# First layer's attentions on one Trainium2 core: score and value products in longer stretches of one kind

## The reference, cut to what matters

```python
def _attn(xq, xc, Wq, Wk, Wv, Wo, bo):
    ...
    scores = jnp.einsum('bnhd,bshd->bhns', q, k) * scale
    attn = jax.nn.softmax(scores, axis=-1)
    out = jnp.einsum('bhns,bshd->bnhd', attn, v).reshape(B, N, HEADS * D_HEAD)
    return out @ Wo + bo
...
x = _attn(_ln(x, g1, b1), _ln(x, g1, b1), Wq1, Wk1, Wv1, Wo1, bo1) + x
x = _attn(_ln(x, g2, b2), context, Wq2, Wk2, Wv2, Wo2, bo2) + x
```

## Time and profile before

| what | value |
|---|---|
| median of the timed runs | 3437.53 us |
| span of the profiled execution, first to last instruction | 3432.5 us |
| PE busy | 3202.0 us, 93% of the span |
| DVE busy | 2266.1 us, 66% |
| ACT busy | 1823.8 us, 53% |
| POOL busy | 1087.6 us, 32% |
| mean granted TensorE clock | 0.957 of full speed |
| `attend_wide`, self | from 184.7 us (first maxima) to 558.1 us (last denominators) |
| `attend_wide`, cross | from 961.5 us (first maxima) to 1984.7 us (last values) |

### The profile page before, as it was taken

One profiled execution on the slowest core, in us unless ns is written; L12 is line 12 of the kernel. 1 busy time (PEld: TensorE's weight loads), 2 busy tenths in 40 slices (PEclk: granted clock), 3 DMA queues, 4 the chain that ended last, 5 costly groups with the idle time before them and its releaser, 6 DMA issues. The chain is left out here.

```text
span 3432.5 us, 48146 instructions
## 1 busy us (share of the span) xinstructions
PE 3202.0 (93%) x17084; PEld 1837.0 (54%) x17084; DVE 2266.1 (66%) x4098; ACT 1823.8 (53%) x3369; POOL 1087.6 (32%) x537
## 2 busy tenths in 40 slices
PE   7969996999979999999999989979999699999989
PEld 5834443888834444444444457733468444444347
DVE  5447774444357666666666555569766599999844
ACT  4424444444424444444444434447766268888864
POOL 1036663000037777777777720002200000000000
PEclk9979998999979999999999999979999789999999
DMA  6888884999785766676667442154544723323140
GB/s 233 306 201 222 227 216 176 362 346 352 281 206 132 160 152 141 140 162 150 142 141 162 117 162 105 71 171 132 193 172 167 251 71 107 104 90 113 59 142 28
DMA packets 367126, 588.79 MB, mean 172 GB/s; under 512 B 47152, under 2 KB 197216, under 8 KB 365736
## 3 DMA queue, kind: packets, MB, share of 16 engines
q1 hardware_dynamic: 361710, 582.41, 57.4%
q10 hardware_dynamic: 5178, 3.31, 0.4%
HBM read 344.19 MB, written 241.29 MB: 171 GB/s over the span
## 5 line engine op out<-in xcount | busy, mean ns | idle before, releaser
L2253 ACT ACTIVATE a_prob<-a_ring 128x512 f32<-128x512 f32 (+1 forms) x1088 | 575.4, 601 | 656.8 <-PE a_ring L2161 587.4
L2279 DVE TENSOR_REDUCE a_blk_max<-a_ring 128x1 f32<-128x402 f32 x1024 | 519.4, 567 | 321.2 <-PE a_ring L2145 321.1
L1790 ACT ACTIVATE a_prob<-a_ring 128x512 f32<-128x512 f32 (+1 forms) x1088 | 582.1, 605 | 136.3 <-PE a_ring L1712 131.1
L2102 POOL TENSOR_TENSOR a_prob_sum<-a_prob,a_prob_sum 128x1024 f32<-128x1024 f32 x256 | 600.6, 2385 | 3.1 <-ACT a_prob L2253 3.1
L2174 PE MATMUL a_pv<-a_prob,a_v 128*64 128x512 f32 (+1 forms) x2176 | 534.5, 610 | 0.0
L1835 DVE TENSOR_REDUCE a_blk_max<-a_ring 128x1 f32<-128x402 f32 x1024 | 506.7, 567 | 33.4 <-PE a_ring L1699 27.0
L2160 PE MATMUL a_ring<-a_q_stack,a_k_stack 128*128 128x512 f32 (+1 forms) x1088 | 463.4, 426 | 13.5 <-DMA a_q_second<-maxima 13.4
L2161 PE MATMUL a_ring<-a_q_second,a_k_second 65*128 65x512 f32 (+1 forms) x1088 | 435.2, 400 | 0.0
L2102 POOL TENSOR_TENSOR a_prob_sum<-a_prob 128x1024 f32<-128x1024 f32 x128 | 302.7, 2375 | 416.7 <-DVE a_chunk_sum L2310 242.7
L1730 PE MATMUL a_pv<-a_prob,a_v 128*32 128x256 f32 (+2 forms) x4096 | 340.7, 406 | 13.6 <-ACT a_prob L1790 7.8
L1699 PE MATMUL a_ring<-a_k_stack,a_q_stack 63*128 63x402 f32 (+1 forms) x1280 | 281.9, 423 | 39.2 <-DMA a_q_stack<-q_lo_self 18.7
(11 more groups left out here) (268 smaller groups left out, 4676.3 us busy)
## 6 DMA issues: line engine op xcount, KB each, us to landing
a_k_stack<-k_hi_cross SPq DMA_DIRECT2D x96, 400.5 KB, 4.6
a_v<-v_cross SPq DMA_DIRECT2D x48, 768.0 KB
a_k_stack<-k_lo_cross SPq DMA_DIRECT2D x80, 400.5 KB, 6.0
a_k_second<-k_hi_cross SPq DMA_DIRECT2D x32, 801.0 KB, 12.5
v_cross<-p_v_sb SPq DMA_DIRECT2D x48, 512.0 KB
k_hi_cross<-p_split_hi SPq DMA_DIRECT2D x120, 200.0 KB, 3.4
k_lo_cross<-p_split_lo SPq DMA_DIRECT2D x120, 200.0 KB, 4.3
a_q_stack<-q_hi_self SPq DMA_DIRECT2D x64, 256.0 KB, 4.2
```

Source lines behind the costliest of these rows:

```text
L1790: nc.scalar.activation(prob[0:keys, tau % RC, m, :], ring[0:keys, score_place(e) % BANKS, :], ACT.Exp, scale=a.scale).then_inc(exp_done, 1)
L2102: nc.gpsimd.tensor_tensor(prob_sum[:, h], prob_of(i * NCP + cp, h), other, ALU.add)\
L2253: nc.scalar.activation(prob_of(w, h)[0:keys, ch % 2, :], ring[0:keys, score_bank(e), :], ACT.Exp, scale=a.scale).then_inc(exp_done, 1)
L2279: nc.vector.reduce_max(dst, ring[:, max_bank(g), 0:a.blk], AX.X).then_inc(item_read, 1)
```

## The change

In the cross attention a group's seven units are put together in four **stints**: `[0]`, `[1, 2]`, `[3, 4]`, `[5, 6]`, that is two, four, four and three chunks. In the self attention one stint holds the whole group (four chunks). PE runs all scores of a stint, then two pairs of maxima, then the values of the stint before, denominators when due, and the rest of the maxima. `a_prob` holds four units in the cross attention too. ACT, DVE and SP get programs in the same order; in the self attention the first loads of maxima (of groups 0 and 1) are now issued by SP. Places that are no longer fitted to units but to stints: `raw_copy` and `high_part` on ACT, and on DVE everything between the maxima reductions.

```diff
-    RC = 3 if a.cross else 4
-    OS = 3 if a.cross else 4
+    RC = 4
+    OS = 2 if a.cross else 4
+    RB = 1 if a.cross else 2
...
+    stints = [[0], [1, 2], [3, 4], [5, 6]] if a.cross else [[0, 1]]
+    NM = len(stints)
+    NS = NG * NM
+
+    def units(k):
+        return [k // NM * NCP + cp for cp in stints[k % NM]]
+
+    def pairs_by(k):
+
+        ahead_by, ramp = ((10, 14, 18, 22), 6) if a.cross else ((8,), 8)
+        steady = PAIRS * (k // NM + 1) + ahead_by[k % NM]
+        return min(NG * PAIRS, steady, PAIRS + ramp * (k + 1))
+
+    def cut(k):
+
+        return min(pairs_by(k), pairs_by(k - 1) + 2)
...
+            if not a.cross:
+                store_maxima(1)
+                load_maxima(1)
+
...
-                    at(store, i - 3)
+                    at(store, i - 2)
...
+            for k in range(NS):
+                for w in units(k):
+                    for ch in a.pair(w % NCP):
+                        for h in range(2):
+                            scores(w, ch % 2, h)
+                maxima(pairs_by(k - 1), cut(k))
+                if k:
+                    for w in units(k - 1):
+                        values(w)
+                sums_at(k)
+                maxima(cut(k), pairs_by(k))
+            for w in units(NS - 1):
+                values(w)
+            if not a.cross:
+                sums_at(NS)
...
-                if not a.cross and cp == NCP - 1 and i + 1 < NG:
+                if not a.cross and cp == NCP - 1 and 1 <= i < NG - 1:
                     load_maxima(i + 1)
...
-                if not a.cross and cp == NCP - 2 and i + 1 < NG:
+                if not a.cross and cp == NCP - 2 and 1 <= i < NG - 1:
                     store_maxima(i + 1)
...
+            def behind_scores(k):
+                if not a.cross:
+                    at(low_part, k - 2)
+                elif k % NM == 1:
+                    at(last_sum, k // NM - 1)
+                    at(last_merge, k // NM - 1)
+                elif k % NM == 3:
+                    at(invert, k // NM - 1)
+                    at(divide, k // NM - 1)
+
+            def behind_values(k):
+                if not a.cross:
+                    at(turn_sums, k - 1)
+                    at(invert, k - 1)
+                    at(divide, k - 1)
+                elif k % NM == 2:
+                    at(turn_sums, k // NM - 1)
+                elif k % NM == 3:
+                    at(low_part, k // NM - 1)
...
+            for k in range(NS + NM + (0 if a.cross else 1)):
+                if k < NS:
+                    blocks(pairs_by(k - 1), cut(k))
+                behind_scores(k)
+                if k < NS:
+                    blocks(cut(k), pairs_by(k))
+                behind_values(k)
```

More of the change, by code:

```diff
@@ L2176, in values, with sums_at @@
                     last.then_inc(pv_done, 1)
-            def sums_at(w):
-                if w >= DEN_AT and (w - DEN_AT) % NCP == 0 and (w - DEN_AT) // NCP < NG:
-                    denominators(pe, (w - DEN_AT) // NCP)
-            maxima(0, pairs_by(-1))
[L2183 to L2195, removed]
+            def sums_at(k):
+                if a.cross and k >= 6 and k % NM == 2:
+                    denominators(pe, (k - 6) // NM)
+                elif not a.cross and k:
+                    denominators(pe, k - 1)
+            maxima(0, pairs_by(-1))
+            for k in range(NS):
+                for w in units(k):
+                    for ch in a.pair(w % NCP):
[11 more added lines that the diff above has]
+                sums_at(NS)
         @block.scalar
@@ L2234, in _ @@
                 i, cp = divmod(w, NCP)
-                if cp == 1 and i:
+                if a.cross and cp == 1 and i:
                     raw_copy(i - 1)
+                elif not a.cross and cp == 0 and i >= 2:
+                    raw_copy(i - 2)
                 if ahead and w - NCP in ahead.early:
@@ L2254, in _ @@
                                              ACT.Exp, scale=a.scale).then_inc(exp_done, 1)
-                if not a.cross and cp == NCP - 2 and i + 1 < NG:
+                if not a.cross and cp == NCP - 2 and 1 <= i < NG - 1:
                     store_maxima(i + 1)
+                if cp == NCP - 1 and a.cross and i:
+                    high_part(i - 1)
+                elif cp == NCP - 1 and not a.cross and i >= 2:
+                    high_part(i - 2)
+            if not a.cross:
+                raw_copy(NG - 2)
+                high_part(NG - 2)
             raw_copy(NG - 1)
-            for i in range((T - 1 - HIGH_AT) // NCP + 1, NG):
-                high_part(i)
+            high_part(NG - 1)
         @block.vector
@@ new lines, in behind_values @@
+            def behind_values(k):
+                if not a.cross:
+                    at(turn_sums, k - 1)
[5 more added lines that the diff above has]
+                    at(low_part, k // NM - 1)
+                if ahead and k < NS:
+                    for m in ahead.early:
+                        if m + NCP in units(k):
+                            ahead.rest_of_piece(dve, m)
+                if ahead and k == NS - 1:
+                    for m in ahead.late:
+                        ahead.rest_of_piece(dve, m)
```

43 lines of the change are left out of this document (16 added, 27 removed).

## The result

The changed kernel takes 3674.74 us in the median of four runs (3669.04 to 3689.43), against 3437.09 us of the kernel before beside it: a ratio of 1.0694, interval 1.0667 to 1.0721. That is 238 us slower, where 62 were forecast, and above the range. The profiled execution has a span of 3676.8 us, 244.3 more than before. One timed run of a kernel further down (experiment 4) took 9234 us; the interval given for that kernel leaves it out.

What follows compares the result with a forecast made beforehand. PE's own sequence was taken to set the pace: +6 us in the cross attention, +61 in the self attention and -5 at the stage ends make +62 on 3437.5, so 3499 us, with 3455 to 3580 for 8 in 10.

Steps and rivals of the forecast that it cites:

- The direction and the two places: Slower, chance 0.86, with PE waiting for DVE's reductions in the cross attention and ACT's store in the self attention.
- The gain in the cross attention: Fewer runs of scores, values and maxima on PE save 42 us together (35.5 and 6.4).
- The wait behind the additions: Cross attention: PE waits 1.6 us for reductions behind last_sum and last_merge in 30 groups, 48 us.
- The wait in the self attention: PE waits all of ACT's store-to-load time at the second pair of maxima, 3.2 us a group, +61 us.
- L: Self attention: time from ACT's store of the maxima to its load, taken as 3.2 us, nearer to the k transfers.
- The clock falls: Rival: half clock behind each self attention wait costs 2.3 us a group, 64 us, giving 3563 us; chance 0.22.
- the last of the signs of being wrong: The forecast is wrong if the clock in the self attention shows half speed in most groups.
- The start of the self attention: SP sends group 1's maxima instead of ACT; PE's wait there taken as unchanged, 0, between -8 and +8 us.
- POOL's additions: At 75% busy in the cross attention, costed at nothing; would bind only if a group became a quarter shorter.
- The end of the stage: PE's 4.68 us wait for POOL's last sums ahead of the last denominators goes, -4.7 us.
- The store passing the loads: Rival: in the self attention ACT's store passes the loads, store to load 2.5 us, +42, 3479 us; chance 0.16.
- the hidden round trip: Rival: the self attention's store-to-load wait costs PE nothing, a group takes 9.69 us, total 3410 us; chance 0.10.

Runs made afterwards that it cites:

- experiment 4: Changed kernel with only last_sum moved early, behind the reductions of stint [0], in the cross attention, last_merge left in place; 3657.25 us, ratio 1.0644 against the kernel before.
- experiment 1: Changed kernel with last_sum and last_merge moved on DVE behind the reductions of the next group's stint [0] in the cross attention; 3547.82 us, ratio 1.0331 against the kernel before.
- experiment 2: Changed kernel with ACT's load of the maxima moved behind the second unit's exponentials in the self attention; 3523.83 us, ratio 1.0254 against the kernel before.
- experiment 7: Kernel with both additions early and load moved, plus one constant reduction of 1.9 us holding DVE in the cross attention; 3449.51 us, one run.
- experiment 8: Changed kernel with SP holding the self attention's loads of k, q and second operands until the maxima of two groups before are loaded; 3608.92 us, one run.
- experiment 3: Changed kernel with both last_sum and last_merge early (cross attention) and the load of the maxima moved later (self attention); 3404.83 us, ratio 0.9919 against the kernel before.
- experiment 6: Kernel with both additions early and load moved, plus two constant reductions, 2.6 us together, holding DVE in the cross attention; 3525.43 us, one run.

## Why the prediction was wrong

- **The direction and the two places** were right: the stall of PE behind DVE's additions in the cross attention and the wait for ACT's store in the self attention are the causes; experiments 1 and 2 take each away by moving one step and get 120 and 152 us of their stages back.
- **The gain in the cross attention**, forecast at 42 us, is 31.28 - 30.11 = 1.17 us a group, 37 us: 5 too high, the mechanism right.
- **The wait behind the additions**, forecast at 1.6 us in 30 groups, was 1.35 in 29. Right within its bounds (1.3 to 1.8).
- **The wait in the self attention**, forecast at 3.2, was 3.34 in the mean, by two errors that cancel: L was 4.47, not 3.2 (the choice nearer to the k transfers was wrong; before the change too the mean was 4.76), and PE waits not for all of L but for L - 0.9 (4.40 and 3.49 in the group above): it goes on when the fifth block is read and not the sixth, 0.6 earlier, and it comes to that item 4.5 after the first score and not 4.25. So the size came out right by luck. With it a group would take 12.9, +61 us.
- **The step that failed** is the price of PE's two waits: the sum took their length alone and put the clock behind them at nothing. "The clock falls" stood only as a rival, with a chance of 0.22, for the self attention alone, on the reading that a wait of 2.21 is borne and one of 4.42 is not. In the changed kernel half clock followed all 29 waits in the self attention, the shortest of 1.03 and 1.04 us too, and in the cross attention 26 of the 29 of 1.35. The price that the rival gave, 2.3 us a group and 64 in all, is what the self attention paid (67); half speed in most groups is also the last of the signs of being wrong that the forecast named. In the cross attention the forecast let no clock fall at all, and 66 us went there. With 67 and 66 on top of 62 the sum is 195 of the 244 us.
- **Of the remaining 49**, 27 lie in the self attention (150 less 67 and the 56 forecast there), 17 in the cross attention (89 less 66 and 6) and 5.5 in the rest of the program. The start of the self attention is one part: 0 was taken, between -8 and +8, and the waits for the first rows of maxima went from 6.6 (before, below) to 14.8 us.

```profile
PE a_ring L2160 <- DMA a_q_second<-maxima: 6.6, 1, 6.6
```

  Others are the 5 us that the cross attention's gain fell short, perhaps a restart behind each wait that the sum left out (with the 0.32 of experiment 7 for each of the 58 waits an estimate of 19 us), and the waits behind POOL (6.4 us). What is left isn't told apart.
- **POOL's additions** were costed at nothing, as they would bind only if a group got shorter by a quarter. That looked at how long they take and not at when they may begin: `last_merge` sets that, and the change moved it. In the changed kernel the error was hidden behind another wait; experiment 4 brought it out.
- **The end of the stage** came as forecast: the 4.68 us for POOL are gone from the list of waits.
- **The store passing the loads** (0.16) and **the hidden round trip** (0.10) did not happen. The forecast gives the sum for the first once as 3478; it is 3479 (3437.5 + 42).

## What to carry to other kernels

A step that makes PE wait is to be priced as the wait, the restart and a possible stretch at half clock, and the last may be as large as the wait itself; whether it comes is not read from other waits of the same kernel. Longer runs of one kind are worth what the run overheads say (here 37 us in the cross attention), provided that every step between them on the other engines is moved to where its engine stands idle: the same order of products was 6.9% slower and, with the additions, the load and the high part moved, 1.7% faster. And an engine that is not busy all the time can still be late, if the step that lets it begin has been moved.

## What the runs showed of the hardware that was not expected

The length of a PE wait does not by itself say whether the clock falls, and neither does its place. Inside a run of scores of the cross attention, 0.72 us left it at full speed in 29 groups (experiment 7), and 1.35 to 1.38 us let it fall in most, but not in all: in the changed kernel 3 of the 29 groups had the same wait of 1.35 among the same products and kept full clock. In the self attention, between two pairs of maxima with the values behind them, waits of 1.03 to 1.5 us were followed by half clock in 16 of 18 cases (experiment 8).

Ahead of the denominators, with the values just done, more was borne. Experiments 2, 3, 6 and 7 have the same program there; from 240 us on none of their 46 waits for `low_part` of up to 1.90 us (the last group left out) was followed by half clock. At 2 us it went either way: of six waits between 1.99 and 2.03 us four were, two were not. Two of the same length, first from experiment 2, then from experiment 6:

```profile
402.71 1.19 PE L2133 MATMUL a_sums<-a_chunk_sum,ones 128*64 128x512 f32 x4 [2.01 <-DVE a_o_lo L2343]
403.83 1.22 PE L2155 MATMUL a_ring<-a_k_stack,a_q_stack 64*128 64x512 f32 x4
```

```profile
417.29 1.08 PE L2133 MATMUL a_sums<-a_chunk_sum,ones 128*64 128x512 f32 x4 [2.01 <-DVE a_o_lo L2343]
418.30 0.73 PE L2155 MATMUL a_ring<-a_k_stack,a_q_stack 64*128 64x512 f32 x4
```

The four maxima behind the wait take 1.22 in the first, at half clock, and 0.73 in the second, at full clock. What decides was not tried.
